# A decoder layer on one core: the up layer's two products in one step of four tiles, four column groups in the down layer, and a new order of steps

## The reference

```python
x = x + L0_attn(layernorm(x))          # FFT of k, v, q; cumsum over rows of k*v; times conj(q); normalised; inverse FFT
x = x + L0_xattn(layernorm(x), ctx)    # 16 heads of 64, causal, ALiBi, softmax, output projection
x = x + L0_ffn(layernorm(x))           # two "Kronecker expert" layers, up and down

def kmoe(x_flat, W_router, A, B, scale, bias, d_in1, d_in2, d_out1, d_out2, top_k):
    logits = x_flat @ W_router.T
    vals, idx = jax.lax.top_k(logits, top_k)
    probs = jax.nn.softmax(vals, axis=-1)
    xs = x_flat.reshape(-1, d_in1, d_in2)
    Y = jnp.einsum('nkoi,nij,nkpj->nkop', A[idx], xs, B[idx])
    return jnp.einsum('nkop,nk->nop', Y, probs).reshape(-1, d_out1 * d_out2) * scale + bias
```

## Time and profile before

| | |
|---|---|
| time, median of 3 runs | 1412.85 us (1409.89 to 1414.78) |
| profiled execution | 1414.63 us, span 1412.7 us |
| granted TensorE clock, mean | 0.969 of full speed |
| PE busy | 1317.5 us, 93% |
| DVE busy | 1102.0 us, 78% |
| ACT busy | 1081.2 us, 77% |
| POOL busy | 772.4 us, 55% |

### The profile page before, as it was taken

One profiled execution on the slowest core, in us unless ns is written; L12 is line 12 of the kernel. 1 busy time (PEld: TensorE's weight loads), 2 busy tenths in 40 slices (PEclk: granted clock), 3 DMA queues, 4 the chain that ended last, 5 costly groups with the idle time before them and its releaser, 6 DMA issues.

```text
span 1412.7 us, 48697 instructions
## 1 busy us (share of the span) xinstructions
PE 1317.5 (93%) x15442; PEld 1056.5 (75%) x15442; DVE 1102.0 (78%) x4099; ACT 1081.2 (77%) x3126; POOL 772.4 (55%) x2382
## 2 busy tenths in 40 slices
PE   6799999999999999999999999999999999998654
PEld 5667787877778787777878777777878777776544
DVE  1366879797987979798897979789797979888543
ACT  2457797878879697887979788897978788796732
POOL 3113647474755737375573747466473737555453
PEclk9899999999999999999999999999999999999666
DMA  9100000000000000000000000000000000000000
GB/s 287 29 16 1 17 3 17 10 10 17 10 17 3 17 10 18 9 10 17 2 17 10 17 10 11 17 10 18 2 17 10 17 10 10 10 2 10 2 9 9
DMA packets 18577, 26.04 MB, mean 18 GB/s; under 512 B 2194, under 2 KB 17171, under 8 KB 18067
## 3 DMA queue, kind: packets, MB, share of 16 engines
q1 hardware_dynamic: 18322, 22.93, 5.5%
HBM read 18.73 MB, written 4.19 MB: 16 GB/s over the span
## 4 chain that ended last, share of the span: by engine, by line
PE 53%; DVE 24%; issue 12%; ACT 4%; DVEq 2%; POOL 2%; POOLq 1%; ACTq 0%
PE P L713 8%; DVE chosen_up L336 6%; PE P L681 4%; PE X L768 4%; PE PT L768 4%; PE P L670 3%; PE G L849 3%; DVE probs L986 3%; PE F L838 3%; PE PT L733 3%; PE G L807 3%; PE X L755 3%; PE P L692 2%; PE F L867 2%; DVE chosen_dn L350 2%
## 5 line engine op out<-in xcount | busy, mean ns | idle before, releaser
L336 POOL COPY chosen_up<-experts 32x128 f32 x1024 | 358.1, 350 | 157.1 <-issue 91.9
L350 POOL COPY chosen_dn<-experts 64x64 f32 x1024 | 222.8, 273 | 198.3 <-issue 179.6
L573 ACT ACTIVATE probs<-probs,neg_max 128x128 f32<-128x128 f32 (+1 forms) x512 | 226.3, 444 | 115.4 <-DVE neg_max L986 114.3
L336 ACT COPY chosen_up<-experts 32x128 f32 x512 | 151.5, 296 | 28.7 <-PE G L849 19.7
L336 DVE COPY chosen_up<-experts 32x128 f32 x512 | 163.0, 318 | 12.7 <-issue 4.2
L986 DVE CUSTOM_DVE_ANT_0 probs<-S,distance 128x128 f32<-128x128 f32 (+1 forms) x512 | 151.7, 351 | 14.8 <-PE S L727 13.5
L733 PE MATMUL PT<-ident,probs 128*128 128x128 f32 x768 | 135.5, 285 | 7.8 <-DVE probsT L993 4.5
L612 ACT ACTIVATE hT<-h 64x1024 f32<-64x1024 f32 x64 | 126.6, 1979 | 6.7 <-DVE h L1114 5.4
L1004 DVE TENSOR_TENSOR probs<-probs,rinv 128x768 f32<-128x768 f32 x128 | 127.1, 993 | 4.4
L692 PE MATMUL P<-wv,ctxT 128*128 128x256 f32 x512 | 122.4, 382 | 0.1
L681 PE MATMUL P<-ctxT,wk 128*128 128x256 f32 x512 | 122.4, 382 | 0.0
(11 more groups left out here) (131 smaller groups left out, 2948.5 us busy)
## 6 DMA issues: line engine op xcount, KB each, us to landing
x<-in_x SPq DMA_DIRECT2D x16, 256.0 KB, 2.7
ctxT<-in_ctxT SPq DMA_DIRECT2D x16, 256.0 KB, 2.7
out<-x2b SPq DMA_DIRECT2D x16, 256.0 KB, 2.2
experts<-in_experts_up SPq DMA_DIRECT2D x2, 1024.0 KB, 19.2
wk<-in_xWk SPq DMA_DIRECT2D x1, 1024.0 KB
wo<-in_xWo SPq DMA_DIRECT2D x1, 1024.0 KB
wv<-in_xWv SPq DMA_DIRECT2D x1, 1024.0 KB, 7.6
wq<-in_xWq SPq DMA_DIRECT2D x1, 1024.0 KB, 9.7
```

Source lines behind the costliest of these rows:

```text
L336: last = copy(to[row:row + D1, n * 2 * F1:(n + 1) * 2 * F1], experts_up[k][:, bass.ds(held[g % LOADED, unit], 2 * F1)])
L350: last = copy(dst, src.rearrange("p (m c) -> p m c", m=2))
L573: act.activation(probs[:, e % 4, lo:hi], probs[:, e % 4, lo:hi], ACT.Exp, bias=neg_max[:, e % 4, rt:rt + 1], scale=-1.0, accum_out=rsum[:, ...
```

## The change

Three edits in one.

First, `first` and `second` become one step, `up`, with nine parts. Part v holds the second product of pair v - 1 and the first product of pair v, token by token in alternation (part 0 has a first product only, part 8 a second one only). The second product now goes crosswise: rows 0 to 63 write partitions 64 to 127 of G and the other way round, so the four products of a token position use the four 64 x 64 tiles of the array, with F and G as targets. The halves of the tokens are swapped at the input (`own_parts`, `choose_up`, `keep_up`), so that the results lie where they lay before. `up` waits for all that `first` waited for and for all that `second` waited for before its first matmul.

Second, `dn_second` spreads its 32 matmuls over four groups of 32 columns instead of two; G's result is therefore in 128 partitions, and `y_keep` makes two copies (64 x 128 each) where it made one (64 x 256).

Third, `ORDER` is another list, with 285 words instead of 292, and it begins at another point of the cycle. Among much else, in the part from the last up product to `score.0` the PE steps were `wo.0 wo.1 turn2 k.1 logits_dn.0-3 ln3_turn fold q.0 q.1 spread_dn` and are `wo.0 wo.1 turn2 logits_dn.0-3 fold q.0 ln3_turn spread_dn`; `x1.0` and `x1.1` stand behind `pre.7` instead of ahead of it; `ln1` stands behind `weights_dn` instead of ahead of `top_dn`; `x2_bias` on POOL stands just ahead of `ln2_root`; `load_ctx`, `v.0`, `v.1`, `k.0`, `cumulate`, `product_q` and `Q` are taken one turn later by the list's count, as it is cut elsewhere.

```diff
-F_USERS = ("ln3_turn", "first", "dn_first", "y_turn")
-G_USERS = ("logits_up", "spread_up", "second", "router_dn", "spread_dn", "dn_second", "y_turn")
+F_USERS = ("ln3_turn", "up", "dn_first", "y_turn")
+G_USERS = ("logits_up", "spread_up", "up", "router_dn", "spread_dn", "dn_second", "y_turn")
...
-            return dst[:, k, il], src[:, half]
+            return dst[:, k, il], src[:, 1 - half]
...
-                row = half * F1 + k * D1
+                row = (1 - half) * F1 + k * D1
...
-            def first(c, v):
...
-            def second(c, v):
...
+            def up(c, v):
+
+                if v < UP_PAIRS:
+                    take_f("up", v, c)
+                    if v == 0:
+                        pe.wait_ge(own_act, at(c, 8, 8))
+                        pe.wait_ge(own_dve, at(c, 8, 8))
+                    for name in CHOOSERS:
+                        pe.wait_ge(chosen[name][0], at(c, UP_GROUPS, 2 * v + 2))
+                w = v - 1
+                if w >= 0:
+                    take_g("up", v, c)
+                    wait_f(pe, "up", w, c)
                 for p in range(UP_TOK):
+                    m, a, b, one = v * UP_TOK + p, 2 * p * F1, (2 * p + 1) * F1, slice(p * F1, (p + 1) * F1)
+                    halves = [slice(half * F1, (half + 1) * F1) for half in range(2)]
+                    if v < UP_PAIRS:
+                        for rows in halves:
+                            mm = pe.matmul(F[rows, one], own[rows, m * F1:(m + 1) * F1],
+                                           chosen_up[v % UP_SLOTS][rows, b:b + F1], start=True, stop=True)
+                        if p == UP_TOK - 1:
+                            mm.then_inc(first_done[0], 1)
+                    if w >= 0:
+                        for rows, other in zip(halves, halves[::-1]):
+                            mm = pe.matmul(G[other, one], W_up[w % 2][rows, one],
+                                           chosen_up[w % UP_SLOTS][rows, a:a + F1], start=True, stop=True)
+                        if p == UP_TOK - 1:
+                            mm.then_inc(second_done[0], 1)
...
-                for u in range(DN_TOK // 2):
+                for odd in (0, 1):
                     for k in range(TOPK):
-                        n = u * TOPK + k
-                        for j in (0, 1):
-                            y = G[j * D1:(j + 1) * D1, 0:DN_TOK * D1].rearrange("p (e u o) -> p u e o", e=2, o=D1)
-                            mm = pe.matmul(y[:, u], W_dn[:, (j * 8 + n) * D1:(j * 8 + n + 1) * D1],
+                        for u, j in ((odd, 0), (odd, 1), (odd + 2, 0), (odd + 2, 1)):
+                            n = u * TOPK + k
+                            to = (u // 2 * 2 + j) * D1
+                            y = G[to:to + D1, 0:4 * D1].rearrange("p (e u o) -> p u e o", e=2, o=D1)
+                            mm = pe.matmul(y[:, u % 2], W_dn[:, (j * 8 + n) * D1:(j * 8 + n + 1) * D1],
...
-                rows = DN_TOK * 4
-                dve.tensor_copy(yT[:, :, i * rows:(i + 1) * rows].rearrange("p d (n r) -> p n r d", r=4),
-                                G[0:F1, 0:DN_TOK * D1].rearrange("p (n r d) -> p n r d", r=4, d=8)).then_inc(g_kept, 1)
+                to = yT[:, :, :].rearrange("p d (i e w s) -> p i w e s d", i=DN_PAIRS, e=2, w=2)
+                for w in range(2):
+                    last = dve.tensor_copy(to[:, i, w], G[w * F1:(w + 1) * F1, 0:4 * D1].rearrange("p (e s d) -> p e s d", e=2, d=8))
+                last.then_inc(g_kept, 1)
```

More of the change, by code:

```diff
@@ L64 @@
 ORDER = """
[L65 to L84, removed]
@@ L85 @@
-choose_act.4@2 cumulate dn_first.3@3 second.0@2 dn_weigh.3@3 choose_act.5@2 choose_act.6@2 exp.4@1 pv.2@1 score.5@1
-choose_dve.6@2 pre.0@2 scale.4@1 choose_pool.6@2 catch_a.3@1 keep_out.2@1 first.1@2 choose_dve.7@2 weigh.1@2
-dn_second.3@3 turn_b.3@1 catch_b.3@1 v_keep.3@1 f_keep.2 y_keep.3@3 v.0 turn_a.4@1 second.1@2 mask.5@1 exp.5@1
-first.2@2 pv.3@1 product_q pre.1@2 catch_a.4@1 weigh.2@2 choose_pool.7@2 choose_dve.8@2 choose_act.7@2 keep_out.3@1
-scale.5@1 score.6@1 y_turn@3 final@3 turn_b.4@1 v.1 catch_b.4@1 first.3@2 second.2@2 choose_act.8@2 cross.1 mask.6@1
@@ L90 @@
[L90 to L94 removed]
+v_keep.3@2 cumulate@1 choose_dve.9@3 keep_out.3@2 pv.4@2 choose_act.7@3 up.3@3 choose_act.8@3 choose_act.9@3
@@ new lines @@
+choose_dve.12@3 inverse@1 choose_act.15@3 keep_out.6@2 choose_dve.13@3 choose_dve.14@3 catch_a.7@2 up.6@3
+choose_dve.15@3 weigh.6@3 pre.5@3 turn_b.7@2 catch_b.7@2 up.7@3 pre.6@3 k_keep.2@1 weigh.7@3 power@1 pv.7@2 root@1
+up.8@3 keep_out.7@2 pre.7@3 x1.0@1 ln2_stats.0@1 x1.1@1 x2_bias@3 ln2_stats.1@1 ln2_root@1 ln2.0@1 ln2.1@1 wo.0@2
+wo.1@2 x2.0@2 x2.1@2 turn2@1 gelu@3 router_dn@3 logits_dn.0@3 load_x logits_dn.1@3 logits_dn.2@3 logits_dn.3@3
+ln3_stats@2 ln3_root@2 ln1_stats ln3@2 xnT2@1 part@3 fold@3 q.0@1 ln3_turn@2 top_dn@3 gap_dn@3 weights_dn@3
@@ new lines @@
+f_keep.1 turn_a.2@1 catch_a.2@1 v_keep.1@1 dn_first.3@3 score.4@1 exp.3@1 own_dve@2 choose_act.2@2 turn_b.2@1 v.2@1
+choose_act.3@2 keep_out.1@1 y_keep.2@3 dn_weigh.3@3 choose_dve.4@2 mask.4@1 catch_b.2@1 dn_second.3@3 up.0@2 exp.4@1
+v_keep.2@1 scale.3@1 k.3@1 pv.2@1 turn_a.3@1 catch_a.3@1 weigh.0@2 product_kv y_keep.3@3 score.5@1 choose_pool.2@2
+choose_pool.3@2 choose_pool.4@2 choose_pool.5@2 choose_pool.6@2 choose_dve.5@2 scale.4@1 y_turn@3 choose_dve.6@2
+keep_out.2@1 turn_b.3@1 catch_b.3@1 v.3@1 final@3 store@3 mask.5@1 choose_dve.7@2 up.1@2 pv.3@1 k_keep.3@1 turn_a.4@1
@@ L605, in gelu @@
             def gelu(c):
-                wait_g(act, "second", UP_PAIRS - 1, c)
+                wait_g(act, "up", UP_PAIRS, c)
                 after(act, parts_done, c)
```

53 lines of the change are left out of this document (23 added, 30 removed).

## The result

The changed kernel takes **1400.78 us** (median of 5 runs, 1399.86 to 1404.07) against 1414.54 (1409.89 to 1418.91) before: a ratio of 0.991, 95% interval 0.9883 to 0.9937. The sign was right. The gain is 13.8 us where 28.5 were forecast, so the forecast of 1384 is 16.8 us short.

What follows compares the result with a forecast made beforehand. PE was full throughout, with DVE nearly full in the 64.9 us stretch B, which the change would leave to DVE. Fourteen turns at 1.85 us (25.9) plus 2.6 in the tail gave 28.5 less: 1384 us, range 1357 to 1415.

Steps and rivals of the forecast that it cites:

- The sign: Whole kernel: faster, with a chance of 0.75; same 0.10, slower 0.15.
- the four tiles: Merged `up` and `dn_second`: a group of four costs 0.0575 us like a pair, saving PE 4.95 us per turn.
- stretch A: From the end of the last `pre` to `keep_dn`: falls from 15.8 to 14.0 us per turn.
- B: Rest of the turn after stretch A, 64.9 us before: 64.85 forecast, PE's work there 62.6.
- the front: Start of stretch A, from the last `pre` to `gelu`: 0.5 us of the 0.6 gap saved.
- Rival 3: Groups of four do not overlap as pairs do, making the kernel slower: 1439 us at 115 ns; chance 0.14.
- B 64.85 ... DVE is last: In B, DVE's terms sum to -0.05 us, giving 64.85; PE needs 63.5, so DVE ends last.
- +0.85 for `pre.7`: In B, `pre.7` waits for `up.8`, which waits for `weigh.7`: 0.85 us more idle DVE per turn.
- -0.4 for `catch_b`: In B, DVE's wait at `catch_b` for PE's late turn goes: 0.4 us less per turn.
- Rival 2: Merged step's waits eat the gain: two more of nine links show 0.85 us, 1408 us; chance 0.15.
- Rival 1: PE stays the end of B and DVE's load gives way: B 63.5, turn 77.5, 1365 us; chance 0.22.
- The tail: Behind the fourteen turns: four `dn_second` save 2.6 us; the last `up`s gain nothing.

Runs made afterwards that it cites:

- light_both: Changed kernel with half of the attention's scaling and most of `weigh` and `pre` left out on DVE: 1370.13 us, ratio 0.9685 to the kernel before.
- experiment 4: DVE work left out: changed kernel without half the scaling (1377.42 us), most of `weigh` and `pre` (1388.82), both (1370.13); kernel before without half the scaling (1401.08).
- experiment 6: Changed kernel with fifth POOL slot and earlier `final` and `store`, plus DVE gathers moved to ACT, five variants: 1391.56, 1390.83, 1390.47, 1389.03, 1388.2 us.
- experiment 3: Changed kernel, against `up.1` waiting for `final` and POOL's gathers for `up.1`: fifth POOL slot (1397.33 us), `final` and `store` earlier (1400.03), both (1393.65).
- light_before: Kernel before the change with half of the attention's scaling on DVE left out: 1401.08 us, ratio 0.9903.

## Why the prediction missed

- **Right: the four tiles, and stretch A.** Groups of four cost 0.05 to 0.06 us as a pair does (0.0575 forecast), `dn_second` 0.58 (0.55). PE's turn fell by 4.1 of the 4.95; in B it is busy 63.26 and not 62.6 (63.04 in the cut of the experiments, where `light_both`, which hardly waits, has 62.57). A is 14.2 (14.0): the front moved by 0.3 and not by 0.5, as ACT's table load now sets `gelu`. Rival 3 is out. The Trainium skill, "TensorE: Matmul & The Clock Gate", section "Wait — 56ns, not 53.3ns?", has starts no closer than about 25 ns; four starts in 60 ns are 15 ns on the average, so the trace disagrees for tiles in different parts of the array.
- **The step that failed: "B 64.85 ... DVE is last", the sum of DVE's terms.** Its idle time was to grow by 0.45 (+0.85 for `pre.7`, -0.4 for `catch_b`); it grew by 2.3 (3.89 to 6.20). The `pre.7` term itself was met (0.87), and experiment 4 shows that `gelu` doesn't feel it, as the table load ends later. What was left out: `pre.6` 0.57, `weigh` 0.43, the Fourier product 0.8 behind POOL, `y_keep` 0.2 behind `dn_second`. The links were priced as if only one of them showed, and POOL's lateness at nothing. On the busy side the sum forecast -0.5 and the trace has -1.36. There `y_keep` cost more than forecast, and the gathers less:

```profile
L335 DVE COPY chosen_up<-experts 32x128 f32 x512 | 144.3, 282 | 11.3 <-issue 1.3
...
L1139 DVE COPY experts<-G 64x128 f32<-64x128 f32 x128 | 48.6, 379 | 7.5 <-PE G L882 4.8
```
```profile
L336 DVE COPY chosen_up<-experts 32x128 f32 x512 | 163.0, 318 | 12.7 <-issue 4.2
```

  Two copies of 379 ns for one of 595 are 0.65 a turn and not 0.4: half the elements took 64% of the time. The 32 gathers a turn fell from 318 (second fence, before) to 282 ns: 1.15 us that I had not seen coming and for which no run shows the cause. Idle +1.86 and busy -0.86 against the forecast make the 1.0 us by which B missed.
- **Rival 2 had the mechanism, but not its whole form.** I priced links one by one at 0.85. The experiments show no fixed price per link: in experiment 4 work left out of DVE shortens B by about half of it, on the links or off them, down to nearly PE's 62.6; in experiment 6 work handed to another engine gives 0.1 to 0.2; experiment 3 shows the ring through POOL as one wait among these. How much of experiment 4's gain is DVE's and how much POOL's stays open. Rival 1 (1365) would have been that floor plus 0.9: the floor is real (63.1 in `light_both`), but only with 5.5 us less on DVE and 2.8 on POOL.
- **The view that misled.** "DVE is last" took B as the longer of two sums. Before, B stood 0.9 above PE's busy time because PE was the one that was full: `light_before` won back 0.6 of that. Once a turn had 4 us less for PE, the two stood at 63 and 60 in 65.85: neither sum was the length of the stretch, as each of the two queues waited for the other by turns.
- **The tail.** Of the 2.6 us for `dn_second` 1.3 came, as three of the four ran at 1.2 GHz, and the `dn_first` between them lost 1.7 in the same way. PE is given less to do there, and its clock was granted less; that the one made the other was not tested. So the account of the profiled executions is: of 25.9 forecast for fourteen turns 11.2 came, 14.7 short (and some 3.5 of the 11.2 are the two long turns of the trace before, luck and not the forecast's doing); the tail is 2.8 short; the start gave 1.2 that nobody had counted. 16.3 in all, of 28.5.

## What to carry to other kernels

When a change takes work from the fullest engine, don't stop at "the next engine's sum": where two in-order engines hand data to and fro, add both idle times as well, and look which of them the cheaper step makes visible. Find the floor by halving the second engine's work in a kernel that leaves some out, look whether a third engine got faster by it, and take the result as the most that an order or a shift of work can win. Try a cheaper step only with a new order: in the old one each cheaper step here made the kernel slower.
